# A fused four-stage kernel (RWKV, mixture of experts, linear attention, ternary FFN): new order at the head, in the slots and at the first tiles, routing weights made once, pad writes on two queues

## The reference

```python
x = _layernorm(x + _L0_attn_ref(x, ...))   # RWKV: k, v, r projections, a scan over the tokens, sigmoid gate, Wo
x = _layernorm(x + _L0_ffn_ref(x, ...))    # top 2 of 8 experts of width 176, weights = softmax of the two logits
x = _layernorm(x + _L1_attn_ref(x, ...))   # linear attention, 16 heads
x = _layernorm(x + _L1_ffn_ref(x, ...))    # FFN with ternary weights
```

```python
router_logits = x_flat @ gate_w.T
top_w, sel = jax.lax.top_k(router_logits, TOPK)
top_w = jax.nn.softmax(top_w, axis=-1)
```

## Time and profile before

| | |
|---|---|
| median of 3 runs | 400.77 us (400.18 to 407.91) |
| the profiled execution's own time | 400.25 us |
| its span, first to last instruction | 398.4 us |
| mean granted TensorE clock | 0.975 |
| busy share of the span: PE, DVE, ACT, POOL | 91%, 73%, 53%, 34% |

### The profile page before, as it was taken

The page is one execution under the profiler, slowest core; times in us unless marked ns, Lnnn a source line. Parts: engine busy times, 40 slices in busy tenths (PEclk is TensorE's granted clock), DMA queues, the critical chain, the costliest instruction groups (busy, mean ns, idle before and its releaser), DMA issues.

```text
span 398.4 us, 7791 instructions
## 1 busy us (share of the span) xinstructions
PE 361.3 (91%) x2440; PEld 323.8 (81%) x2440; DVE 292.1 (73%) x748; ACT 210.5 (53%) x483; POOL 137.4 (34%) x233
## 2 busy tenths in 40 slices
PE   8999999999598999999999847999999999999790
PEld 8999889998476877767777736999999999999680
DVE  6996999999974584895453264797879788876741
ACT  6664677668555333355335414556555564646451
POOL 4001077776717520030310268244536240311201
PEclk9999999999789999999999998999999999999986
DMA  7899411111234357533521131102021100000000
GB/s 224 299 307 243 145 55 41 40 55 54 75 99 133 120 176 247 147 105 101 153 81 53 54 92 54 53 2 81 10 73 33 48 29 0 28 2 26 0 28 26
DMA packets 28567, 35.79 MB, mean 90 GB/s; under 512 B 3696, under 2 KB 25712, under 8 KB 28272
## 3 DMA queue, kind: packets, MB, share of 16 engines
q1 hardware_dynamic: 19696, 21.78, 18.4%
q0 software_dynamic: 3072, 8.39, 6.6%
q10 hardware_dynamic: 5760, 5.12, 3.9%
HBM read 22.83 MB, written 12.45 MB: 89 GB/s over the span
## 4 chain that ended last, share of the span: by engine, by line
PE 49%; DVE 34%; issue 8%; ACT 4%; POOL 3%; DMA 1%; ACTq 0%; DVEq 0%; POOLq 0%
PE bank L414 19%; PE bank L558 10%; PE bank L579 8%; DVE st L1110 4%; PE bank L750 2%; PE bank L424 2%; PE bank L695 2%; PE bank L538 2%; PE bank L568 2%; DVE arena L1599 2%; DVE arena L1592 2%; DVE arena L1173 2%; DVE arena L1197 1%; DVE arena L1494 1%; ACT arena L1073 1%
## 5 line engine op out<-in xcount | busy, mean ns | idle before, releaser
L812 ACT ACTIVATE arena<-bank 128x256 f32<-128x256 f32 (+1 forms) x118 | 45.3, 422 | 40.1 <-PE bank L579 28.9
L1688 POOL TENSOR_TENSOR ve<-mv,eps 128x2 f32<-128x2 f32 x32 | 8.1, 252 | 158.8 <-DVE mv L1114 111.5
L558 PE MATMUL bank<-gu,arena 128*128 x156 | 52.6, 460 | 0.0
L817 ACT ACTIVATE arena<-arena,nm,rs 128x256 f32<-128x256 f32 x48 | 26.2, 596 | 39.8 <-POOL nm L1696 39.6
L1772 POOL DMA_INDIRECT arena<-yg,ypos x32 | 31.2, 974 | 38.9 <-DMA yg<-arena 30.4
L579 PE MATMUL bank<-dn,arena 96*128 x156 | 41.1, 385 | 2.4 <-DVE arena L1370 2.4
L1370 DVE COPY arena<-bank 96x256 f32<-96x256 f32 x39 | 16.3, 419 | 33.3 <-PE bank L568 32.9
L1742 POOL DMA_INDIRECT xg<-x,pos x32 | 35.4, 1107 | 14.3 <-issue 7.3
L579 PEld LDWEIGHTS bank<-dn,arena 96*128 96x128 f32 x156 | 28.6, 190 | 11.9 <-issue 4.3
L414 PE MATMUL bank<-arena 128*128 128x256 f32 (+2 forms) x192 | 34.3, 321 | 3.4 <-DVE arena L1185 1.9
L414 PE MATMUL bank<-x_hi,w1q 128*128 128x256 f32 x128 | 36.0, 305 | 1.5 <-ACT x_hi L812 1.5
(11 more groups left out here) (275 smaller groups left out, 1120.0 us busy)
## 6 DMA issues: line engine op xcount, KB each, us to landing
arena<-xg SPq DMA_DIRECT2D x39, 128.0 KB, 2.1
yg<-arena ACTq DMA_DIRECT2D x39, 128.0 KB, 1.7
arena<-in_xT SPq DMA_DIRECT2D x8, 256.0 KB, 5.9
...
```

Source lines behind the costliest of these rows:

```text
L558: last = pe.matmul(bank[BANK_GU[i % 2]][:, 0:2 * F], xtT[:, i % 2, chunk(k)], w[:, :, k, :, bass.ds(e, 1), :], start=k == 0, stop=k == KC - 1)
L812: return act.activation(dst, src, ACT.Copy)
L817: last = act.activation(dst[:, t, :], src[:, t, :], ACT.Identity, bias=nm[:, i, t:t + 1], scale=rs[:, i, t:t + 1])
```

## The change

- Head: 11 warming matmuls for 16. ACT and DVE round the first half of Wk, then x, then the second half; PE's first keys are a new function, `first_keys`, whose 24 matmuls are ordered by the part that they need, with a wait ahead of each group. `xs_high(1)` and `xs_low(1)` stand later.
- Slots: PE's projections are split in two halves. `output(s - 1)` stands ahead of the (second half of the) values, `rank` between the halves of the gates. In slot 6 (batch 4 is routed) PE turns x1 inside the keys, ACT copies it first, DVE chooses between its multiplication and its scans, and positions and `first_places` stand ahead of the last scan; `tile_order` stands in that slot too.
- Tiles: DVE's `tile_places` stands ahead of `exponents(7)`, `tile_table` right behind it. `turn_x1(5)` and `logits(5)` stand around `output(6)`, ahead of `turn(0)`. ACT takes the norm of batch 5 first, that of batch 6 between the evacuation and the store of tile 0. DVE's statistics of batches 6 and 7 stand behind hidden products. POOL makes the deviations of batches 6 and 7 ahead of and between the scatters of batch 5.
- The routing weights are made once for all batches, by one ACT instruction behind tile 12 and three POOL instructions. `odds`, `gaps` and `weights` are gone; `mx8` and `gap` hold all 16 token tiles.
- Pads: SP writes four of the eight; ACT writes the other four, one behind each of the tiles 5 to 8. SP waits for all eight, as before.

```diff
-WARM = 16
+WARM = 11
...
-            for e in range(E):
+            for e in range(E // 2):
                 r0 = sp.value_load(table[0:1, T_PAD + e:T_PAD + e + 1], min_val=e * REGION, max_val=e * REGION + NTOK)
                 sp.dma_start(xg[bass.ds(r0, P), :], zero[:, :]).then_inc(pad_ok, 16)
             sp.wait_ge(table_ok, 2)
             sp.wait_ge(scat2_ok, 16 * 2 * NT * (B - FULL_AT))
-            sp.wait_ge(pad_ok, 16 * E)
+            sp.wait_ge(pad_ok, 16 * (E // 2))
+            sp.wait_ge(pad2_ok, 16 * (E // 2))
...
-                    pe.wait_ge(wlow_ok, j + 1)
-                for d in range(KC):
+                    pe.wait_ge(wlow_ok, j + 2)
+                for d in parts:
...
+                pe.wait_ge(xsh_ok, 1)
+                pe.wait_ge(whigh_ok, 2)
+                add(wA_hi, xs_hi, 0, first=True)
+                pe.wait_ge(wlow_ok, 1)
+                add(wA_lo, xs_hi, 0)
+                pe.wait_ge(whigh_ok, 4)
+                add(wA_hi, xs_hi, 1)
+                pe.wait_ge(xsl_ok, 1)
+                add(wA_hi, xs_lo, 0)
+                add(wA_hi, xs_lo, 1)
+                pe.wait_ge(wlow_ok, 2)
+                add(wA_lo, xs_hi, 1, final=True).then_inc(kp_mm, 1)
...
             def a_slot(s):
                 old, now, new = s - 2, s - 1, s + 1
-                if 0 <= new < B:
+                value_bank = halves(1 + new % 2)
+                if new == 0:
+                    first_keys(halves(0))
+                else:
                     past(pe, ku_ok, new)
-                    project(new, 0, halves(0), kp_mm)
-                if 0 <= old < B:
-                    turn_x1(old)
-                if 0 <= new < B:
-                    past(pe, cv_ok, new - 1)
-                    project(new, 1, halves(1 + new % 2), vp_mm)
-                if 0 <= old < B:
+                    project(new, 0, halves(0), kp_mm, (0,))
+                    if old == FULL_AT - 1:
+                        turn_x1(old)
+                    project(new, 0, halves(0), kp_mm, (1,))
+                past(pe, cv_ok, new - 1)
+                if old == FULL_AT - 1:
                     logits(old)
-                if 0 <= now < B - 1:
-                    output(now)
-                if old == FULL_AT - 1:
+                    project(new, 1, value_bank, vp_mm, (0,))
                     rank(old)
                     first_total()
-                if 0 <= new < B:
-                    past(pe, gate_ok, new)
-                    project(new, 2, halves(3), rp_mm)
+                elif 0 <= old:
+                    turn_x1(old)
+                    project(new, 1, value_bank, vp_mm, (0,))
+                    logits(old)
+                if 0 <= now:
+                    output(now)
+                project(new, 1, value_bank, vp_mm, range(1 if 0 <= old else 0, KC))
+                if old == FULL_AT - 1:
+                    tile_order(0, bank[7][:, 4 * E:4 * E + 1])
+                past(pe, gate_ok, new)
+                project(new, 2, halves(3), rp_mm, (0,))
                 if 0 <= old < FULL_AT - 1:
                     rank(old)
+                project(new, 2, halves(3), rp_mm, (1,))
...
-            tile_order(0, bank[7][:, 4 * E:4 * E + 1])
             tile_rows(0, bank[7][:, 8 * E:8 * E + 2 * FIRST], where1[:, :, :])
+            turn_x1(B - 3)
             output(B - 2)
-            turn_x1(B - 3)
+            logits(B - 3)
...
-            logits(B - 3)
...
-            weights_high(0)
+            weights_high(0, (0,))
             xs_high(0)
+            weights_high(0, (1,))
             weights_high(1)
             weights_high(2)
-            xs_high(1)
...
+                if old == FULL_AT - 1:
+                    copy_x1T(old)
...
+                if s == -1:
+                    xs_high(1)
...
+            def pad(e):
+                if e == E // 2:
+                    act.wait_ge(zero_ok, 1)
+                    act.wait_ge(pads_ok, 1)
+                r0 = act.value_load(table[0:1, T_PAD + e:T_PAD + e + 1], min_val=e * REGION, max_val=e * REGION + NTOK)
+                act.dma_start(xg[bass.ds(r0, P), :], zero[:, :]).then_inc(pad2_ok, 16)
+
+            normalise_x1(B - 3)
             exponents_high(B - 1)
+            copy_x1T(B - 3)
             gate_exponentials(B - 1)
-            normalise_x1(B - 3)
-            copy_x1T(B - 3)
             turned(0)
             turned(1)
             reciprocal(B - 1)
             act.preload_act_table_set("silu_and_others")
+            silu(0)
             turned(2)
-            silu(0)
             silu(1)
             turned(3)
-            gaps(B - 3)
+            silu(2)
+            evacuate(0)
             normalise_x1(B - 2)
-            tile(0)
+            turned(4)
+            store(0)
             copy_x1T(B - 2)
             tile(1)
-            gaps(B - 2)
             tile(2)
             normalise_x1(B - 1)
             copy_x1T(B - 1)
             tile(3)
-            gaps(B - 1)
...
                 tile(i)
+                if 5 <= i < 5 + E // 2:
+                    pad(i - 5 + E // 2)
+                if i == 12:
+                    odds()
...
+                if s == 0:
+                    xs_low(1)
...
-                states(s)
-                if 0 <= old:
+                if old == FULL_AT - 1:
+                    weighted_values(s)
                     choose(old)
-                if 0 <= now:
-                    residual(now)
-                if old == FULL_AT - 1:
+                    weights_state(s)
                     positions(old)
                     dve.wait_ge(pos_ok, old)
                     dve.wait_ge(route_step, 4 * old + 4)
                     dve.tensor_copy(pos[:, tiles_of(old), :], pos_f[:, tiles_of(old), :]).then_inc(pos_ok, 1)
                     first_places()
+                    values_state(s)
+                else:
+                    states(s)
+                    if 0 <= old:
+                        choose(old)
+                if 0 <= now:
+                    residual(now)
...
-            exponents(B - 1)
             dve.wait_ge(asked_ok, valid_at[0])
             tile_places(0, where1, bank[7][:, 4 * E:4 * E + 1])
+            exponents(B - 1)
+            tile_table(0, bank[7][:, 8 * E:8 * E + 2 * FIRST])
             differences(B - 1)
-            tile_table(0, bank[7][:, 8 * E:8 * E + 2 * FIRST])
             finish_y(B - 2)
...
+            def spread(b):
+                statistics(0, x1[:, tiles_of(b), :], b + 1)
+
             finish_y(B - 1)
             residual(B - 2)
+            positions(B - 3)
             hidden(0)
-            positions(B - 3)
+            spread(B - 2)
             hidden_turned(0)
             hidden(1)
             residual(B - 1)
+            spread(B - 1)
...
+            for b in range(FULL_AT):
+                deviation(0, b + 1)
+                if b:
+                    scatter(b - 1)
+            scatter(FULL_AT - 1)
+            deviation(0, FULL_AT + 1)
+            deviation(0, FULL_AT + 2)
+            scatter(FULL_AT, (0,))
+            deviation(0, FULL_AT + 3)
+            scatter(FULL_AT, (1,))
+            for b in range(FULL_AT + 1, B):
+                scatter(b)
+
+            pool.wait_ge(route_step, 4 * (B - 1) + 1)
+            pool.tensor_tensor(gap[:, :], mx8[:, :, 1], mx8[:, :, 0], ALU.subtract).then_inc(gap_ok, 1)
+            pool.wait_ge(odds_ok, 1)
+            for j, w in enumerate((-0.5, 0.5)):
+                pool.tensor_scalar(topw[:, :, j], gap[:, :], w, 0.5, ALU.mult, ALU.add)
```

115 lines of the change are left out of this document (45 added, 70 removed).

## The result

| | before | after |
|---|---|---|
| median | 400.77 us | 406.14 us (404.40 to 407.00, 5 runs) |
| ratio to before | | 1.0132, 95% interval 1.0095 to 1.0169 |
| profiled execution, its span | 400.25, 398.4 | 404.40, 402.6 |
| mean granted clock | 0.975 | 0.968 (other executions 0.954 to 0.967) |

The changed kernel is 1.3% slower. I had forecast 401.0, range 396.0 to 403.6: the result lies outside. By the 2% bound it counts as "same", as forecast at 0.94, but its interval excludes no change. Two of its five executions ran at a clock of 0.967 to 0.968 (404.40 and 405.48 us), three at 0.954 (406.14 to 407.00). Now and then an execution of the kernel before also runs at a lower clock (0.954 to 0.956, 406 to 408 us); the ratios leave such ones out.

A forecast was written before the change was run, and what follows sets the result against it. PE is busy 91% of the span; slots run at DVE's pace, tiles at PE's. Lead, pad wait and clock sum as 400.25 - 3.8 + 3.2 + 1.3 = 400.95, say 401.0 us; range 396.0 to 403.6.

The forecast's parts named there:

- 2% bound: Whole kernel: a measurement can tell about 2%, 8 us, from no change; faster 0.03, same 0.94, slower 0.03.
- Head and slots: Start to slot 7: first keys from 6.2, slot 1's 2.90 us wait gone, slot 2 at 34.6, slot 7 at 98.3.
- Slots to tiles: Handover from slot 7 to the first tiles: a lead of 3.8 us, bounds 3.1 and 4.5, output(7) at 112.0.
- The 1.2 us given back at turn_x1(6): Behind output(7): turn_x1(6) waits for a norm that ACT takes only behind tile 0's evacuation, giving back 1.2 us.
- The fall of the clock that I expected at this place: Slots to tiles: PE's idle stretch, 98.6 to 103.5, stays as long as the old one, so the clock falls as before.
- The 1.75 at turn_x1(7) that stays: In the tiles: PE's 1.75 us wait at turn_x1(7) stays, as ACT takes that norm behind tile 2's store.
- Pads: Before turn(13): ACT's last pad holds the load of tile 13, so PE waits 3.2 us, bounds 2.7 and 3.8.
- The fall of the clock in that wait, 1.3: Behind the wait before turn(13): a low clock costs 1.3 us, between 0 for no stretch and 3.4 for two.
- All else "shifts along": Everything behind the tiles: unchanged, and only shifts along in time.
- The slower rival: Tiles: clock low for two stretches behind the wait (3.4), lead only the slots' 3.1, giving 404.0; chance 0.12.

The follow-up runs named there:

- slot1_only: The kernel before with one edit: in slot 1 PE's output product of batch 0 stands ahead of the values' 24 matmuls; 398.04 us, ratio 0.9928.
- pads_split_only: The kernel before with nothing but the pads split, four on SP and four on ACT behind tiles 5 to 8; 406.29 us, ratio 1.0140.

## Why the prediction was wrong

- **Head and slots**: right. First product 6.24 (forecast 6.2); no wait of `residual` in slot 1; no wait of DVE in slots 2 to 6 of the profile; slot 2 at 34.31 (34.6) and slot 7 at 97.89 (98.3) with the pads on SP, 35.43 and 98.98 in the profile of after, where x of batch 2 landed later. That the slots go at DVE's pace was right, and slot1_only shows that the slots' gain is worth 2.8 us at the end.
- **Slots to tiles, the step that failed**: "I take 3.8 us as the lead at this place, bounds 3.1 (only what came from the slots) and 4.5". It was 1.1 (1.9 with pads on SP, whose slots were on time). At output(7) I had 4.5 us of lead (112.0), measured were 2.5, and 3.3 with the slots on time; from there to turn_x1(6) I gave back 0.7 to 1.1 and 1.4 went. Three things of it: (1) POOL's deviation began at 100.58 where I had 99.2 (slots 0.8 us behind the forecast in this execution, the first scatter 1.61 us for 0.96) and took 3.05 for 2.3, so the norm ended at 104.76 for 102.7. (2) I counted what waits for that norm on PE, and not what ACT has queued behind it: the exponentials of batch 7, for which DVE stood 1.13 us. The change moved the norm ahead of them on ACT and turn_x1(5) ahead of output(6) on PE, so a late norm now holds three engines; outputs(7) came at 108.64 for 107.4. The chain from there to output(7), which I had 1.3 us shorter than before (4.6 for 5.9), took 5.3, so output(7) came at 113.93 for 112.0. (3) The 1.2 us given back at turn_x1(6) were right in size (1.23) but came on top of the rest. The fall of the clock that I expected at this place came, and was shorter than before: 0.69 as the mean of 104.8 to 109.3 and 1.00 behind it, where the kernel before had 0.50 from 105.4 to 112.2.
- **The 1.75 at turn_x1(7) that stays**: right, but the low clock that can follow it was not in the sum. That clock was seen in some executions only.
- **Pads**: the mechanism was right, the size a little high. Wait 2.59 for 3.2, just under the bounds of 2.7 to 3.8; load 2.6 us behind ACT's last pad for the 2.7 taken from SP's. The Trainium skill, "DMA: Bandwidth & Descriptors", section "Issuing engines are not separate DMA queues", says that starting DMAs on several engines saves only the sequencer's time. The runs agree (pads split in a good place: 401.97, all on SP: 401.97). By that rule the price would have been 0. What cost here was that ACT came late to its share.
- **The fall of the clock in that wait, 1.3**: 1.5 in the profile of after, 2.8 in pads_split_only. With the wait that makes 4.1 and 5.7 for the forecast 4.5; taking the pads back brought 4.2. As a sum this part was right.
- **All else "shifts along"**: no. The last long wait for ACT (1.46 us, at 378.42 before and 381.59 after) was followed by a low clock until 387.4, not 381.8, which cost 1.0 us.

So: forecast -3.8 + 3.2 + 1.3; measured in the profile -1.1 + 2.8 (turn(13) from 1.1 ahead to 1.7 behind) + 1.5 + 1.0 = +4.2. The median is another 1.7 above the profiled execution (404.40), at a lower clock (0.954); in which stretch those executions lost it is not recorded. The slower rival (404.0, to which I gave 0.12) came near the profiled time by luck: it put the lead at 3.1 us (1.1 measured) and the clock behind the wait at 3.4 (1.5 measured), and the two errors nearly cancel.
